# Layer-norm means and deviations of the feed-forward through rows in memory instead of transposes on TensorE

## What is computed

```python
# per sample b; x1 is the sample after attention, T x C = 512 x 512
def layernorm(x, gamma, beta):
    mu = jnp.mean(x, axis=-1, keepdims=True)        # one mean per token
    var = jnp.var(x, axis=-1, keepdims=True)        # one variance per token
    return (x - mu) * jax.lax.rsqrt(var + EPS) * gamma + beta
h2 = layernorm(x1, gamma2, beta2)
ff = jax.nn.gelu(h2 @ W1 + b1, approximate=False) @ W2 + b2
x2 = x1 + ff
out = x + gate * (x2 - x)
```

## Time and profile before

| | |
|---|---|
| median of 3 runs | 1663.08 us (1661.63 to 1665.82) |
| the profiled execution's own time | 1660.57 us |
| its span in the trace | 1658.8 us |
| PE busy | 1609.5 us, 97% |
| DVE, ACT, POOL busy | 1163.5, 985.5, 397.3 us |
| mean busy share of the DMA engines in queue 1 | 46.8% |

### The profile page before, as it was taken

One profiled execution on the slowest core, in us unless ns is written; L12 is line 12 of the kernel. 1 busy time (PEld: TensorE's weight loads), 2 busy tenths in 40 slices (PEclk: granted clock), 3 DMA queues, 4 the chain that ended last, 5 costly groups with the idle time before them and its releaser, 6 DMA issues.

```text
span 1658.8 us, 27195 instructions
## 1 busy us (share of the span) xinstructions
PE 1609.5 (97%) x9318; PEld 1302.3 (79%) x9318; DVE 1163.5 (70%) x2767; ACT 985.5 (59%) x2329; POOL 397.3 (24%) x606
## 2 busy tenths in 40 slices
PE   6799999999999999999999889999999999999999
PEld 4678777777777767677767678888999999999998
DVE  7799887886868687878778457676565656565643
ACT  5789765987878787777778636343242424242422
POOL 6788700313131313131311110100102020202010
PEclk8899999999999999999999999999999999999999
DMA  7122224644444444444336352856555554646451
GB/s 307 69 76 77 102 107 98 173 117 107 113 108 110 114 114 112 116 116 116 91 91 183 118 203 115 316 210 248 219 191 210 191 236 165 265 147 247 173 203 70
DMA packets 61825, 254.80 MB, mean 154 GB/s; under 512 B 10580, under 2 KB 15956, under 8 KB 45944
## 3 DMA queue, kind: packets, MB, share of 16 engines
q1 hardware_dynamic: 61688, 253.06, 46.8%
HBM read 153.93 MB, written 48.23 MB: 122 GB/s over the span
## 4 chain that ended last, share of the span: by engine, by line
PE 85%; DVE 4%; DMA 4%; ACT 2%; POOL 2%; issue 1%; SPq 1%; DVEq 0%; ACTq 0%; POOLq 0%
PE psum L83 22%; PE psum L84 21%; PE psum L85 21%; PE psum L1692 5%; PE psum L1672 5%; PE psum L1722 5%; DMA k_raw<-in_w_in 1%; PE psum L1613 1%; DMA k_early<-in_w 1%; PE psum L1621 1%; PE psum L1603 1%; PE psum L2627 1%; DMA out<-k_result 0%; DMA k_stack<-k_maxima 0%; PE psum L1708 0%
## 5 line engine op out<-in xcount | busy, mean ns | idle before, releaser
L1359 ACT ACTIVATE psum<-psum,b_mx 128x512 f32<-128x512 f32 (+3 forms) x512 | 258.5, 507 | 61.3 <-DVE b_mx L1102 59.1
L1102 DVE CUSTOM_DVE_ANT_0 psum<-psum,b_mask 128x512 f32<-128x512 f32 (+3 forms) x512 | 243.1, 509 | 71.6 <-PE psum L1672 64.7
L2573 ACT ACTIVATE k_act<-k_stack_f,k_smalls 128x512 f32<-128x512 f32 x112 | 81.0, 723 | 337.4 <-DVE k_stack_f L2411 337.4
L1371 ACT ACTIVATE k_exps<-psum 128x512 f32<-128x512 f32 (+1 forms) x384 | 196.4, 530 | 71.7 <-PE psum L1692 70.3
L976 POOL TENSOR_SCALAR_AFFINE_SELECT k_exps<-k_exps 128x256 f32<-128x256 f32 x256 | 97.3, 417 | 388.9 <-ACT k_exps L1371 388.9
L2390 DVE TENSOR_TENSOR k_act_lo<-k_act,k_act_hi 128x512 fp32r<-128x512 f32 x112 | 77.4, 691 | 130.5 <-ACT k_act_hi L2576 128.9
L2271 POOL TENSOR_SCALAR k_result<-k_result,k_pb 128x512 f32<-128x512 f32 x32 | 58.4, 1839 | 431.5 <-DVE k_result L2330 431.5
L83 PE MATMUL psum<-k_act_hi,k_w_hi 128*128 128x512 f32 x384 | 151.0, 393 | 2.0 <-DVE k_act_lo L2383 1.5
L84 PE MATMUL psum<-k_act_lo,k_w_hi 128*128 128x512 f32 x384 | 150.7, 392 | 0.0
L85 PE MATMUL psum<-k_act_hi,k_w_lo 128*128 128x512 f32 x384 | 150.2, 391 | 0.0
L2411 DVE TENSOR_TENSOR k_raw<-psum,k_raw 128x256 f32<-128x256 f32 x168 | 70.7, 421 | 104.5 <-PE psum L85 98.0
(11 more groups left out here) (377 smaller groups left out, 4420.9 us busy)
## 6 DMA issues: line engine op xcount, KB each, us to landing
k_stack<-w_factors SPq DMA_DIRECT2D x35, 1792.0 KB, 7.6
k_stack<-k_samples SPq DMA_DIRECT2D x384, 128.0 KB, 2.4
k_weights<-w_factors SPq DMA_DIRECT2D x17, 1792.0 KB, 7.7
x<-k_tokens SPq DMA_DIRECT2D x10, 1024.0 KB, 3.9
k_tokens<-x SPq DMA_DIRECT2D x8, 1024.0 KB, 5.6
d<-k_result SPq DMA_DIRECT2D x32, 256.0 KB, 2.9
k_raw<-x SPq DMA_DIRECT2D x8, 1024.0 KB, 4.8
k_raw<-d SPq DMA_DIRECT2D x8, 1024.0 KB, 7.1
```

The costliest lines, as they stand in the source:

```text
L1102: last = dve.tensor_tensor_reduce(got, got, mask[:, S - width:S], -INV_SQRT_DH, -2.0 * MASKED, ALU.add, ALU.min, mx[n % 2][:, h, t:t + 1])
L1359: act.activation(sc(n, u)[:, at:at + width], sc(n, u)[:, at:at + width], ACT.Exp, bias=mx[n % 2][:, h, t:t + 1], scale=-1.0, accum_out=sum ...
L1371: act.activation(exps[n % 2][:, h, at:at + width], by_key(n, u)[:, 0:width], ACT.Exp, scale=INV_SQRT_DH).then_inc(k_act, 1)
L2573: act.activation(act_f[:], whole_tile, ACT.Gelu, bias=small(smalls, "b1", 2 * pair % M + second)).then_inc(pair_gelu, 1)
```

## The change

The 48 transposes of `spread` go. In their place SP's new `rows_through(b)` stores `mv[:, :, 0]` and `rstd` into a small tensor `rows` in device memory, in the order of the tokens (a store of 128 x 4 single elements of 4 bytes each), waits until both have landed, and loads each row of 512 numbers back, repeated to all 128 partitions (128 x 2 KB = 256 KB each), into the eighth rows of the first two ring places, which the factors (seven rows) leave free. `centre` and `normalise` wait for these loads and read the rows there. DVE's next `statistics` waits until the stores have read `mv`. `tokens` of the next sample waits for the last statistics instead of for the last `normalise`. The three semaphores (`w_ld`) are those that counted the loads of the attention weights at the start, used on.

`rows_through(2)` stands behind `factors_in(5)` in SP's list; for the five samples b + 2 = 3 to 7, the fourth to the eighth, it stands right behind a factor load in period 4 of the loop over n.

```diff
@@ -2116,6 +2116,7 @@
     whole_tile = keep["stack_f"][1][:, 7, :]
     partial = rows_of(keep["raw"][:, 2:4, :, :])[:, 6:8, :].rearrange("p n (h s) -> p (n h) s", h=2)
     u2, u3 = (partial[:, n, :] for n in (2, 3))
+    mean_row, rstd_row = keep["stack_f"][0][:, 7, :], rows_of(keep["raw"][:, 0:2, :, :])[:, 7, :]
     beside_first = partial[:, 0:2, :]
     beside_0 = rows_of(keep["weights"][:, 2:4, :, :])
     beside_1 = late("h1", [P, 2 * FACTORS, S], F32R, H1)
@@ -2132,6 +2133,8 @@
     h_set, sum_set, h_hi_set, h_lo_set = sem("h_set"), sem("sum_set"), sem("h_hi_set"), sem("h_lo_set")
     hidden_full, gelu_set, act_hi_set, act_lo_set = sem("hidden_full"), sem("gelu_set"), sem("act_hi_set"), sem("act_lo_set")
     added, summed, biased, gated = sem("added"), sem("summed"), sem("biased"), sem("gated")
+
+    row_st, mean_ld, rstd_ld = keep["w_ld"]
     given_ld, factor_sum, factor_hi, factor_lo = sem("given_ld"), sem("factor_sum"), sem("factor_hi"), sem("factor_lo")
     factor_st, factor_ld = ([sem(f"factor_{n}{k}") for k in range(count)] for n, count in (("st", 2), ("ld", RING)))
     product_full, copied, partial_set, pair_gelu = sem("product_full"), sem("copied"), sem("partial_set"), sem("pair_gelu")
@@ -2236,6 +2239,18 @@
                 wait_stored(sp, n - RING)
             wait_stored(sp, n % HALF)
             sp.dma_start(as_stored(ring[n % RING]), io["w1_factors"][n % HALF]).then_inc(factor_ld[n % RING], 16)
+
+        def rows_through(b):
+
+            sp.wait_ge(mv_set, T * b)
+            sp.dma_start(io["rows"][b, 0, :, :].rearrange("t p -> p t"), mv[:, :, 0], allow_slow_non_contiguous=True).then_inc(row_st, 16)
+            sp.wait_ge(rstd_set, b)
+            sp.dma_start(io["rows"][b, 1, :, :].rearrange("t p -> p t"), rstd[:], allow_slow_non_contiguous=True).then_inc(row_st, 16)
+            sp.wait_ge(row_st, 16 + 32 * (b - 1))
+            if b > 2:
+                sp.wait_ge(normed, T + 2 * J * (b - 2))
+            for k, (row, ld) in enumerate(((mean_row, mean_ld), (rstd_row, rstd_ld))):
+                sp.dma_start(row, io["rows"][b:b + 1, k, :, :].rearrange("o t p -> o (t p)").broadcast_to((P, S))).then_inc(ld, 16)
 
         def samples():
             factors_in(2)
@@ -2248,6 +2263,7 @@
             pair_in(6)
             factors_out(5)
             factors_in(5)
+            rows_through(2)
             pair_in(7)
             factors_out(6)
             factors_in(HALF)
@@ -2259,6 +2275,8 @@
                 factors_in(n)
                 if b and p == 1 and b + 2 < B:
                     sample_in(b + 2)
+                if b and p == 4 and b + 2 < B:
+                    rows_through(b + 2)
             sample_out(B - 1)
             sp.wait_ge(out_st, 16 * J * B)
 
@@ -2335,6 +2353,8 @@
                 dve.wait_ge(tok_set, t + 1)
             else:
                 dve.wait_ge(tin_full, T * (b - 1) + t + 1)
+            if b > 2 and t == 0:
+                dve.wait_ge(row_st, 16 + 32 * (b - 2))
             dve.bn_stats(st[:, t, :], tok[:, t, :] if b == 1 else turn(t)).then_inc(stat_set, 1)
             dve.wait_ge(stat_set, T * (b - 1) + t + 1)
             dve.bn_aggr(mv[:, t, :], st[:, t, :]).then_inc(mv_set, 1)
@@ -2346,15 +2366,15 @@
                                   ALU.mult).then_inc(normed, 1)
 
         def centre(b):
-            dve.wait_ge(tback_full, J + 2 * (b - 2) + 1)
+            dve.wait_ge(mean_ld, 16 * b)
             for j in range(J):
-                dve.tensor_tensor(tok[:, j, :], x[:, j, :], turn(0), ALU.subtract).then_inc(normed, 1)
+                dve.tensor_tensor(tok[:, j, :], x[:, j, :], mean_row, ALU.subtract).then_inc(normed, 1)
 
         def normalise(b):
-            dve.wait_ge(tback_full, J + 2 * (b - 1))
+            dve.wait_ge(rstd_ld, 16 * b)
             for j in range(J):
                 dve.wait_ge(normed, T + 2 * J * (b - 2) + j + 1)
-                dve.tensor_tensor(tok[:, j, :], tok[:, j, :], turn(1), ALU.mult).then_inc(normed, 1)
+                dve.tensor_tensor(tok[:, j, :], tok[:, j, :], rstd_row, ALU.mult).then_inc(normed, 1)
 
         def block_low(b, i):
             n = FACTORS * (b - 1) + SPLIT_AT[i] + 1
@@ -2617,7 +2637,7 @@
                 elif b == 2:
                     pe.wait_ge(h_set, J)
                 else:
-                    pe.wait_ge(normed, T + 2 * J * (b - 2))
+                    pe.wait_ge(stat_set, T * (b - 1))
             if t >= 2:
                 if b == 1:
                     pe.wait_ge(tok_set, t - 1)
@@ -2634,17 +2654,6 @@
                 pe.wait_ge(h_set, j - 1)
             for t in range(T):
                 last = pe.transpose(turn(j)[:, t * P:(t + 1) * P], tok[:, t, j * P:(j + 1) * P], ident[:])
-            last.then_inc(tback_full, 1)
-
-        def spread(b):
-
-            pe.wait_ge(mv_set, T * b)
-            for t in range(T):
-                last = pe.transpose(turn(0)[:, t * P:(t + 1) * P], mv[:, t, 0:1].to_broadcast([P, P]), ident[:])
-            last.then_inc(tback_full, 1)
-            pe.wait_ge(rstd_set, b)
-            for t in range(T):
-                last = pe.transpose(turn(1)[:, t * P:(t + 1) * P], rstd[:, t:t + 1].to_broadcast([P, P]), ident[:])
             last.then_inc(tback_full, 1)
 
         def first_product(m):
@@ -2719,8 +2728,6 @@
             if more and p == 3:
                 tokens(b + 1, 2)
                 tokens(b + 1, 3)
-            if more and p == 4:
-                spread(b + 1)
             if first:
                 product(n, 4)
                 product(n, 5)
@@ -4032,6 +4039,7 @@
     shape = (B, P, J, S)
     for n in ("x1", "x2", "d"):
         io[n] = nc.dram_tensor(n, shape, F32, kind="Internal").ap()
+    io["rows"] = nc.dram_tensor("rows", (B, 2, T, P), F32, kind="Internal").ap()
     io["w1_factors"] = nc.dram_tensor("w1_factors", (HALF, P, FACTORS * 4 * P), F32, kind="Internal").ap()
     io["out"] = nc.dram_tensor("out", shape, F32, kind="ExternalOutput").ap()
     build(nc, io)
```

## The result

The changed kernel takes 1719.85 us (median of 5, 1717.17 to 1725.82) against 1663.08 us (median of 5). The ratio is 1.0342, with a 95% interval of 1.0328 to 1.0357: 57 us slower, where the forecast was 2 us slower and its range ended at 1680.7. The two profiled executions (1660.57 and 1719.85 us) lie 59.3 us apart.

The account below looks back on a forecast made before the run. PE's instruction stream was taken to bound the stage: 1660.57 + 6.9 us of stalls - 4.7 of transposes = 1662.8 for the profiled execution, 1665.3 us for the median; range 1658.0 to 1680.7.

Parts of the forecast that it names:

- The bound and the gain: PE's instruction stream bounds the feed-forward stretch; removing six groups of transposes gains 4.74 us, 0.28% of the kernel.
- the hidden case: Rival: stores pass the load or cost next to nothing, row there by t = 10.0, only the gain left: 1658.3 us; chance 0.13.
- The queue: DMA queue: stores issued behind a factor load start when that load is through, at t = 7.0, their fixed time hidden.
- s: Time both stores take after the factor load: 64 packets per engine at 27 ns, 1.7 us; bounds 0.2 to 4.8.
- The upper end: Upper bound of s: both stores one behind the other at 2.4 us of a full store alone, 4.8 us, giving 1680.7.
- dear elements: Rival: scattered 4-byte writes cost more per element; slower by over 0.3% from s = 2.27, 1672.7 at 50 ns; chance 0.28.
- The fixed part: The skill's fixed 2.0 us per DMA in place of s would bring the mean row at t = 11.8; set aside.
- t: Time in us from the issue of the factor load right ahead of the stores; mean row forecast at 11.5.
- The row's load: SP's load of the mean row, 256 KB repeated to all partitions: 2.7 us, as `b_mask`, with 2.4 as lower end.
- slow repeated load: Rival: 128 partitions reading the same 2 KB takes twice 2.7 us, row at t = 14.2, 1678.8 us; chance 0.07.
- The third sample: Its mean row comes at 1103.7, before `centre` begins at 1107.0; no stall up to s = 5.
- the formula: Stalls at five samples less the transposes' gain: 5 x (9.8 + s) - 50.6 - 4.74 us.

Follow-up runs that it names:

- no_store: The changed kernel without both stores and SP's wait for them, the row loads reading a constant input: 1658.14 us, ratio 0.9970 to the kernel before.
- best: Changed kernel with statistics transposes taking every fourth token, stores in 16-byte runs, stores and loads ahead of the factor load; second measurement, more rounds: 1659.24 us, ratio 0.9972.
- strided_ahead: Changed kernel with statistics transposes taking every fourth token, stores in 16-byte runs, stores and loads ahead of the factor load; first measurement: 1659.52 us, ratio 0.9956.
- strided: Changed kernel with statistics transposes taking every fourth token and stores in 16-byte runs, stores and loads still behind the factor load: 1668.66 us, ratio 1.0032.
- ahead4: Changed kernel with its two stores and two loads ahead of the factor load in SP's list, single 4-byte elements kept: 1694.62 us, ratio 1.0170.

## Why the prediction was wrong

- **The bound and the gain** were right. PE is the stage's clockwork; without the stores the kernel takes 1658.14 us, forecast for the hidden case 1658.3. The gain by itself came out at 5 to 6 us there and 4.3 to 5.2 in the two runs ahead of the load, 4.7 forecast.
- **The queue** was right: the small packets go out as soon as the factor load's are through (1199 to 1201.5), and a store takes its place in line.
- **The step that failed is s,** the time from the factor load's end to the stores' landing. It was worked out as 64 packets per engine at 27 ns, 1.7 us. The packets took 9 ns each, but the landing came 7.7 us behind the load (5.5 to 9.0 by sample), 8 us of it without a packet at the fourth sample. What makes it long is how densely the 4-byte elements lie in device memory, 16 in 64 bytes: with the same number and size one to 64 bytes s is 1.2 us, below the forecast. The row used for the price, 2 KB transfers of 512-byte pieces into on-chip memory, shows the engines and says nothing of such writes. The upper end, 4.8 us from two full stores, was taken from stores whose pieces of 2 KB share no line; no row bounded the completion of small elements side by side. The rival "dear elements" had the right place and sign, but it too priced each element wherever it goes, and that is not what costs.
- **The fixed part.** The estimate from the Trainium skill was set aside because a store behind a load showed no fixed time. The same section, "Anatomy of one DMA" on the page "DMA: Bandwidth & Descriptors", is written for transfers that GpSimd issues, where these come from SP. It says that the last descriptor waits for the data to be written, and that this "can cause a surprisingly long delay especially when the write target is HBM". The trace agrees so far as it goes: 8 us without a packet on any engine before the landing. Where the time is spent it doesn't show, and the fixed 2.0 us would have given t = 11.8 where 18.4 was measured.
- **The row's load** took 3.3 to 5.5 us (median 3.6) where 2.7 was forecast, and 3.2 where the runs read a constant. The prediction said that the rival "slow repeated load" decides from 3.3 us on. So it was right in part; alone, with s at 1.7, it would have given 5 x 12.4 - 50.6 - 4.7 = 6.7 us, and not 57.
- **The third sample** was said to have room up to s = 5. Its stores, issued from 1098.6 on, landed at 1109.5, 8.2 us behind the factor load (issued at 1093.94, 7.4 us to landing), and `centre` waited 3.85 us there too.
- **From the stall to the time** the formula lacked a term. With the mean row at t = 14.8 + 3.6 = 18.4, the formula gives 5 x 18.4 - 50.6 - 4.7 = 36.7 us, that is 41.4 us of stops. PE in fact waited 44.1 us at the five places (7.9 to 10.7 each) and 2.5 at the third sample. The term that was missing is the clock. PE's busy time in the stretch rose by 10.8 us while 4.7 us of work left it, so the work behind the stops took about 15.5 us more. Against the busy time of the three runs without stops (596.9 to 599.4 us in `no_store`, `best` and `strided_ahead`) it is 12 to 14, so this is an estimate of 12 to 15.5. Busy time times the missing share of the clock, read behind each of the six stops, gives 13. Together, 44.1 + 2.5 + 12 to 15.5 - 4.7 is 54 to 57 of the 59.3 us between the two profiled executions.
- **The same term in the small.** For `strided` the formula gives 5 x 11.3 - 50.6 - 4.7 = 1.2 us, and 5.1 were measured. Some of that is the restart: at the seventh sample 1.84 us lie between the starts of the matmuls before and behind the stop, and the row of the wait counts 1.57. Another part is the clock again. PE's stops are 0.8 to 1.8 us here, and behind the longest, at the fifth sample (1.78 us, to 1290.38), the granted clock was 0.50 for some 3 us:

```profile
1291.00:1293.00 2.00, 2.00 (x7) 1.61 (x6) 0.49 (x1) 1.62 (x3) 0.00 (x0) 0.50 0.57 241
```

  That costs about 1.7 us, an estimate from the busy time and the clock there. Restarts (0.27 us, five times) and clock bring the sum to about 4.2 of the 5.1 us; the rest is within what one execution differs from another.
- **A slip in the rivals.** "Hidden" was called 0.4 us of s away. By the prediction's own terms the row is there by t = 10.0 for s = 0.2, which is 1.5 us below the 1.7 taken.
- **The ends of the range:** 1719.85 lies 39 us above the upper one. The forecast followed from the assumption that the price of a write is the engine's time for it, and its end from stores of another kind.

## What to carry to other kernels

Price a small store by its completion, not by its packets: if someone waits for it, look at how densely its separate elements lie in device memory (here 16 in 64 bytes were slow, two were not). Lay data out so that each partition writes a run (here 16 bytes), or give each element a place of its own, and issue the store ahead of large transfers rather than behind them. And where PE is the bound, a stop of 8 to 11 us cost more than its length here, since the work behind it started at the lower clock.

## What the runs showed of the hardware

- 1024 stores of 4 bytes with 16 in each 64 bytes of device memory land 7.7 us after the transfer ahead of them, the same 1024 with one or two in 64 bytes 1.2 to 1.3 us, and with eight 3.2 us. At the fourth sample of the change no DMA engine has a packet from 1202 to 1209.5 us. It makes no difference whether the elements of 64 bytes come from 4 or from 16 partitions (7.4 and 7.7 us). Over which unit of memory the density counts was not told apart: two elements in 64 bytes, one in each 32, cost nothing, 16 bytes apart was not tried, and units above 64 bytes fit the runs as well. Where the waiting takes place no run shows.
- A store of 2 KB in runs of 16 bytes with nothing ahead of it landed in 1.4 us for the means and 1.7 for the deviations (medians of five in `best`; the first was 2.7 at the seventh sample), and a store of 256 KB in 2.4 us. In single elements with 16 in 64 bytes it took 8.9 us (`ahead4`).
- The factor load itself was reported late in two of five samples of the changed kernel (12.9 and 15.4 us instead of 7.0), with the stores right behind it. Why in these two is open, and no one waited for it.
- After 10.7 us of standstill PE's granted clock was 0.50 and stayed there for the first 5 us of work; after stops of 7.9 and 8.0 us it was 0.50 for the first 2.5. In `strided` it stayed at 1.00 behind a stop of 1.57 us and fell to 0.50 behind one of 1.78 us, and in the changed kernel it was 0.50 from 1118 to 1120 us, 2 us behind a stop of 2.5 us.
- PE's weight loads for the transposes took 209 ns with every fourth token (`best`) in place of 140, and the kernel's time, 4.3 us below the kernel before, doesn't show it.
